# Gated cross-attention block: row maxima split by GpSimd before a single bf16 transpose, two heads later

## What is computed

```python
xn = layernorm(x)
q, k, v = xn @ Wq.T, ctx @ Wk.T, ctx @ Wv.T          # per head, D = 16
p = softmax(where(mask, q @ k.T / sqrt(D), -inf))
x = x + tanh(g_xattn) * ((p @ v) @ Wo.T + bo)
xq = fake_quant(layernorm(x), clip_x)                # one scale for all of x
h = fake_quant(silu(xq @ Wg.T) * (xq @ Wu.T), clip_down)
x = x + tanh(g_ffn) * (h @ Wd.T)
```

## Time and profile before

| | us |
|---|---|
| median of 3 runs | 254.37 |
| lowest and highest of them | 254.21, 257.52 |
| the profiled execution | 256.14 |
| its span, from first to last instruction | 254.6 |
| PE busy | 212.0 |
| DVE busy | 212.6 |
| ACT busy | 160.1 |
| POOL busy | 138.0 |

### The profile page before, as it was taken

How to read it: one execution, slowest core, us unless ns; L and a number is a source line. 1 busy time by engine, 2 the same in 40 slices (tenths; PEclk the granted TensorE clock), 3 DMA queues, 4 the chain that set the end, 5 groups by cost and what they waited for, 6 DMA issues and landing times.

```text
span 254.6 us, 5343 instructions
## 1 busy us (share of the span) xinstructions
PE 212.0 (83%) x1661; PEld 145.1 (57%) x1664; DVE 212.6 (84%) x419; ACT 160.1 (63%) x293; POOL 138.0 (54%) x241
## 2 busy tenths in 40 slices
PE   0899799979989999999999999989592898853970
PEld 0688688857746666666666666645361443312850
DVE  3378699979898998988989898969957779998992
ACT  2347476476687766667677666677726588865920
POOL 7446467643452536285675838389835433330590
PEclk9999999999999999999999999999979599996897
DMA  6999948999546653455436152000000600000296
GB/s 219 236 295 295 299 134 226 272 258 259 145 140 167 130 124 97 102 127 125 128 98 139 45 138 83 4 0 4 1 0 0 206 3 1 0 4 0 25 144 167
DMA packets 34185, 30.80 MB, mean 121 GB/s; under 512 B 5232, under 2 KB 27760, under 8 KB 34160
## 3 DMA queue, kind: packets, MB, share of 16 engines
q1 hardware_dynamic: 29776, 27.74, 40.2%
q0 software_dynamic: 1360, 1.31, 4.2%
q10 hardware_dynamic: 3024, 1.44, 2.1%
HBM read 20.65 MB, written 9.70 MB: 119 GB/s over the span
## 4 chain that ended last, share of the span: by engine, by line
PE 35%; DVE 27%; issue 10%; ACT 9%; POOL 7%; DMA 5%; SPq 4%; ACTq 0%; POOLq 0%; DVEq 0%
PE bank_o L1439 9%; PE bank_a L1422 6%; PE bank_b L1408 4%; PE bank_a L1448 3%; ACT arena L763 3%; DVE h_max L1200 3%; PE bank_a L1325 3%; DMA big<-in_ctx 3%; DVE big L1209 2%; DMA big<-max_parts 2%; DVE arena L1237 2%; DVE arena L902 2%; DVE v_all L1243 2%; POOL big L486 1%; DVE resid L917 1%
## 5 line engine op out<-in xcount | busy, mean ns | idle before, releaser
L912 DVE TENSOR_REDUCE neg_max<-bank_b 128x2 f32<-128x512 f32 x128 | 80.1, 672 | 4.9 <-PE bank_b L1314 3.0
L1422 PE MATMUL bank_a<-big 98*128 98x256 bf16 x256 | 48.8, 274 | 6.2 <-ACT arena L763 2.3
L763 ACT ACTIVATE arena<-bank_a 128x512 f32<-128x512 f32 x64 | 34.3, 605 | 13.9 <-PE bank_a L1422 13.8
L1408 PE MATMUL bank_b<-big 96*128 96x256 bf16 x224 | 42.7, 272 | 0.3 <-issue 0.2
L763 ACT ACTIVATE big<-bank_a 128x512 f32<-128x512 f32 x64 | 33.9, 595 | 12.4 <-PE bank_a L1422 12.1
L1422 PEld LDWEIGHTS bank_a<-big 98*128 98x128 bf16 x256 | 20.2, 97 | 25.4 <-issue 8.8
L1325 PE MATMUL bank_a<-arena,w_t 128*128 128x256 f32 x128 | 30.8, 387 | 0.2 <-issue 0.2
L1325 PEld LDWEIGHTS bank_a<-arena,w_t 128*128 128x128 f32 x128 | 23.6, 194 | 3.6 <-issue 0.6
L510 POOL TENSOR_TENSOR arena<-resid,arena 128x512 bf16<-128x512 f32 x16 | 18.3, 1160 | 10.7 <-ACT arena L701 10.7
L1408 PEld LDWEIGHTS bank_b<-big 96*128 96x128 bf16 x224 | 21.1, 97 | 4.5 <-issue 0.8
L570 POOL TENSOR_TENSOR x_rows<-x_rows,arena 128x256 f32<-128x256 f32 x14 | 11.6, 833 | 15.4 <-ACT arena L772 15.4
(11 more groups left out here) (179 smaller groups left out, 437.7 us busy)
## 6 DMA issues: line engine op xcount, KB each, us to landing
qk_parts<-arena SPq DMA_DIRECT2D x8, 768.0 KB, 5.5
big<-qk_parts SPq DMA_DIRECT2D x32, 192.0 KB, 3.3
big<-qk_parts SPq DMA_DIRECT2D x32, 128.0 KB, 3.3
x_rows<-in_x SPq DMA_DIRECT2D x8, 256.0 KB, 6.3
big<-qk_parts SPq DMA_DIRECT2D x32, 64.0 KB, 3.5
big<-in_ctx SPq DMA_DIRECT2D x7, 256.0 KB, 4.9
out<-x_rows SPq DMA_DIRECT2D x7, 256.0 KB, 2.8
out<-v_all POOLq DMA_DIRECT2D x5, 256.0 KB, 6.3
```

Of the source, the lines that this page charges most:

```text
L763: act.activation(probabilities(h), ring_bank(b, ("exp", h)).rearrange("p (c s) -> p c s", c=QC), ACT.Exp, scale=SCALE).then_inc(exp_done, 1)
L912: dve.tensor_reduce(neg_max[:, p, :, h], bank.rearrange("p (c s) -> p c s", c=QC), axis=AX.X, op=ALU.max, negate=True).then_inc(max_done, 1)
L1408: done = mm(to, q_st[0:KR, p, h, c * P:(c + 1) * P], k_st[0:KR, p, h], start=True, stop=not masked)
L1422: done = mm(to, k_st[0:KM, p, h, k * P:(k + 1) * P], q_st[0:KM, p, h], start=True, stop=not masked)
```

## The change

The split moves ahead of the transpose. GpSimd reads `neg_max` itself (128 rows on the partitions, 8 heads x 2 row halves = 16 values in each) and writes both bf16 parts to `max_parts`, 128 x 32 for a half. For this `neg_max` is laid out by heads, so that the 16 values lie side by side. PE does one bf16 transpose of 128x32 where it did two of f32; ACT copies 32x128 bf16 values to `max_t`; each DMA reads 16 partitions of 256 bytes where it read 8 of 512. The split now waits for DVE's reductions (and for the transpose that read the buffer before), PE waits for the split, ACT for the transpose and SP for ACT's copy. Two waits of GpSimd for the DMAs of the step before are gone. The transposes and copies stand at heads 3 and 11, where they stood at 1 and 9.

```diff
-    PE_AT = {"max_tr": 1, ("pv", 1): H + 1, ("out", 1): 2 * H + 3, "next_max_tr": 9, ("pv", 0): 9,
+    PE_AT = {"max_tr": 3, ("pv", 1): H + 1, ("out", 1): 2 * H + 3, "next_max_tr": 11, ("pv", 0): 9,
              ("out", 0): H + 11}
...
             def max_rows(b, p, half):
-                sp.wait_ge(mp_done, 2 * b + half + 1)
+                sp.wait_ge(mf_done, 2 * b + half + 1)
                 for k in range(2):
                     sp.dma_start(q_st[KR + k:KR + k + 1, p, HH * half:HH * half + HH],
-                                 max_parts[:, half, k]).then_inc(max_in[half], 16)
+                                 max_t[HH * QC * k:HH * QC * (k + 1), half]).then_inc(max_in[half], 16)
...
             def max_split(b, half):
-                pool.wait_ge(mf_done, 2 * b + half + 1)
+                heads = slice(HH * half, HH * (half + 1))
+                pool.wait_ge(max_done, H * b + HH * (half + 1))
+                if b:
+                    pool.wait_ge(mt_done, 2 * b + half - 1)
                 alone(pool)
-                chain.step(pool.tensor_copy(max_parts[:, half, 0], max_f[:, half]))
-                pool.tensor_tensor(max_parts[:, half, 1], max_f[:, half], max_parts[:, half, 0],
+                chain.step(pool.tensor_copy(max_parts[:, half, 0], neg_max[:, b % 2, heads]))
+                alone(pool)
+                pool.tensor_tensor(max_parts[:, half, 1], neg_max[:, b % 2, heads], max_parts[:, half, 0],
                                    ALU.subtract).then_inc(mp_done, 1)
...
-                    act.wait_ge(mp_done, 2 * b + half - 1)
+                    act.wait_ge(max_in[half], 32 * b)
...
-                act.activation(max_f[:, half], src[0:HH, 0:S], ACT.Copy).then_inc(mf_done, 1)
+                act.activation(max_t[:, half], src.bitcast(BF16)[0:2 * HH * QC, 0:P], ACT.Copy).then_inc(mf_done, 1)
...
-                pe.wait_ge(max_done, H * b + HH * (half + 1))
-                for c in range(QC):
-                    done = tr(to[0:HH, c * P:(c + 1) * P], neg_max[:, p, c, HH * half:HH * (half + 1)], ident_f[:])
+                pe.wait_ge(mp_done, 2 * b + half + 1)
+                done = tr(to.bitcast(BF16)[0:2 * HH * QC, 0:P], max_parts[:, half].rearrange("p k h c -> p (k h c)"), ident_b[:])
                 done.then_inc(mt_done, 1)
```

More of the change, by code:

```diff
@@ L104, in flamingo_block @@
               ("rec", 0): 13, ("means", 0): 2 * H + 13, ("back", 0): H + 3}
-    ACT_AT = {"max": 1, ("scaled", 1): 2 * H + 3, "next_max": 9, ("scaled", 0): H + 11}
-    PE_LAST = {"max_tr": 1, ("pv", 1): H + 1, ("out", 1): 2 * H + 2, ("out", 0): H + 6, ("out", 2): H + 7, ("pv", 0): 9}
-    ACT_LAST = {"max": 1, ("scaled", 1): 2 * H + 2, ("scaled", 0): H + 6, ("scaled", 2): H + 7}
+    ACT_AT = {"max": 3, ("scaled", 1): 2 * H + 3, "next_max": 11, ("scaled", 0): H + 11}
+    PE_LAST = {"max_tr": 3, ("pv", 1): H + 1, ("out", 1): 2 * H + 2, ("out", 0): H + 6, ("out", 2): H + 7, ("pv", 0): 9}
+    ACT_LAST = {"max": 3, ("scaled", 1): 2 * H + 2, ("scaled", 0): H + 6, ("scaled", 2): H + 7}
     RING, LAST = ([slot for h in range(H) for slot in (("exp", h), *(what for what, at in places.items() if at % H == h
@@ L155, in flamingo_block @@
         wd_diag = sb("wd_diag", [P, EC, P])
-        neg_max = sb("neg_max", [P, 2, QC, H])
-        max_f = sb("max_f", [HH, 2, S])
-        max_parts = sb("max_parts", [HH, 2, 2, S], BF16)
+        neg_max = sb("neg_max", [P, 2, H, QC])
+        max_parts = sb("max_parts", [P, 2, 2, HH, QC], BF16)
+        max_t = sb("max_t", [2 * HH * QC, 2, P], BF16)
         rec = sb("rec", [P, 2, NB])
@@ L587, in step @@
             def step(b, p):
-                if b:
-                    pool.wait_ge(max_in[1], 32 * b)
                 max_split(b, 1)
@@ L598, in step @@
                     scale_heads(b - 1, 1)
-                pool.wait_ge(max_in[0], 32 * (b + 1))
                 max_split(b + 1, 0)
@@ L619, in _ @@
                 step(b, b % 2)
-            pool.wait_ge(max_in[1], 32 * (B - 1))
             max_split(B - 1, 1)
@@ L911, in maxima @@
                 dve.wait_ge(a_done, H * b + h + 1)
-                dve.tensor_reduce(neg_max[:, p, :, h], bank.rearrange("p (c s) -> p c s", c=QC),
+                dve.tensor_reduce(neg_max[:, p, h], bank.rearrange("p (c s) -> p c s", c=QC),
                                   axis=AX.X, op=ALU.max, negate=True).then_inc(max_done, 1)
```

## The result

The kernel after the change takes 261.34 us (median of 4 runs, 259.33 to 262.54), against 254.80 us for the kernel before on the same chip (4 runs, 254.21 to 257.52). The ratio is 1.0243, with a 95% interval of 1.0187 to 1.03: slower by about 2.4%. The forecast was 255.0 us with a range up to 258.0. The profiled execution took 259.33 us, with a span of 257.7; that of before took 256.14, with 254.6.

A forecast was written before the change was run, and what follows sets the result against it. PE and DVE were busy some 83%; GpSimd's 14.36 us loop was taken to bound later steps, PE's order and transfers earlier ones. 0.28 - 0.33 + 1.35 - 0.25 - 0.25 + 0 - 0.25 = +0.55 on 254.37 gave 255.0 us, range 253.0 to 258.0.

The forecast's parts named there:

- the start: Before step 0: PE's first transpose waits for GpSimd's first split, so PE goes on at 64.36, +0.28 us.
- the copy: ACT's copy of the transposed maxima: falls from 0.36 to 0.25 us, bounds 0.14 and 0.36.
- the split: GpSimd's split of the maxima into two bf16 parts: 0.60 us instead of 1.11, bounds 0.58 and 1.1.
- the chain from transpose to head 8 in step 1: Transpose, exp of head 3, copy 0.25, transfer 2.53: about 3.35 us; head 8 of step 1 +1.60 us.
- the move costs cover at both places: Transposes at heads 3 and 11 stand behind the products with v; cover of 1.8 to 2.7 us, heads 0 and 8 wait.
- The transfer: DMA of the maxima, issue to PE: 2.53 us as before, at most 1.0 more.
- short runs make every transfer slower: Rival at heads 0 and 8: at +0.5 us per transfer, 6.3 us on top, 261.3 us; chance 0.05.
- So 0.25 us comes back: From step 3 GpSimd's loop is the longer; 0.25 us regained, eviction +1.05 in step 3, +0.8 in step 4.
- PE is held by GpSimd: Rival: split keeps 1.14 us, transposes at head 3 come 0.54 later in five steps, 257.4 us; chance 0.13.
- the transposes: PE: two f32 transposes of 0.31 us become one bf16 of 0.06, saving 0.25 each time where PE isn't waiting.
- DVE's chain carries this to the end: Step 7: the first products lose their transposes once more, leaving +0.55 us, which DVE's chain carries to the end.

The follow-up runs named there:

- early split: The change with GpSimd's split of the next second half moved ahead of its Newton steps and normalisation; at heads 1 and 9 with 8 partitions 252.90 us.
- the second set of runs: The change itself, unaltered, measured and traced once more: 262.18 us (ratio 1.0278).
- the early kernel at 1 and 9: The change with GpSimd's split ahead of its Newton steps and normalisation and the transposes back at heads 1 and 9, still 16 partitions: 255.8 us (1.0059).

## Why the prediction was wrong

The forecast failed in two steps, the transfer in step 0, and GpSimd's loop from step 3 on, where 0.25 us were to come back in each of two steps. By its own steps:

- **Right:** the start (the first transpose at 64.30, with PE idle 0.25 for the split, the next product at 64.45 against 64.08, +0.37 where +0.28 was forecast), the copy (0.25), the split (0.60), the chain from transpose to head 8 in step 1 (3.05 us from 88.45 to 91.50, forecast 3.35), the transfer there (2.35, forecast 2.53), and that the move costs cover at both places.
- **Failed: "The transfer" taken as 2.53 us in step 0.** It took 4.6. The forecast bounded it by the landing of other loads, as one price for all places, and did not ask what else the DMA engines carry at the place: in step 0 a store sent 1.8 us before and a fetch of instructions. The rival "short runs make every transfer slower" had the sign (over 2.7 us from issue to PE) in step 0 alone and the wrong cause: with 8 partitions the length of the run is nothing (3.11 us against 3.13), and sixteen partitions took 2.35 in step 1. That its 261.3 us is the measured median is luck. DMA: Bandwidth & Descriptors of the Trainium skill (Specifications) wants at least 512 bytes in a transfer for line rate, and its section Why small descriptors are slow exempts transfers inside SBUF. These runs agree with the exemption, as far as 4 KB can tell: 252.92 us with runs of 256 bytes and 252.90 with 512. The slow transfer and the lost cover make +3.53 at the first eviction where +1.34 was forecast. In runs in which the clock then falls, some 2.8 us more.
- **Failed: "So 0.25 us comes back" in steps 3 and 4, and nothing lost behind them.** Each of steps 3 to 6 lost 0.53 to 0.78. The forecast gave GpSimd's loop its way out by copy and transfer only. It put the projection, heads 4 to 7 and the reductions behind the held transpose, with a few tenths hidden. They are the chain: transpose, projection, eviction, weight row, exp, head 7. Term by term, from eviction to eviction in step 3: to the split's start 5.73 (before 5.70), the split 0.60 (before 1.11), from there to the products 4.45, 117.40 to 121.85 (before 3.80, 114.09 to 117.89), from the products to the eviction 4.11 (before 3.75; one more transpose stands in between now). That is +0.03 - 0.51 + 0.65 + 0.36 = +0.53. That is the rival "PE is held by GpSimd", which was right in mechanism but had the wrong condition: it doesn't need a dear split. At 0.60 for the split it is already there, since what matters is when the split ends, late behind the normalisation, and not how long it takes.
- **Mis-sized: the transposes.** 0.45 us for eight of the feed-forward part, back to back, gave 0.06 for one. Standing alone among other products it holds 0.16 to 0.23 of PE's order (95.33 to 95.49, 117.40 to 117.63). The f32 pair held 0.31 by the starts in the timeline and 0.22 in most places of the chain. So the saving is 0.15 at most and not 0.25.
- **Held by the medians: "DVE's chain carries this to the end."** 6.58 us at step 6 and 6.5 between the medians. The two profiled spans differ by only 3.1, and 2.7 of what is missing is the clock of before's trace.
- **Left out: the clock.** The forecast had granted clock 1.00 throughout and asked of no wait whether it would lower it.

A ledger by the table, in us of the medians: the kernel with nothing but the cheaper work (early split, places 1 and 9, 8 partitions) stands at 252.9, 1.9 under before (254.80). Head 1 to 3 adds 1.4, head 9 to 11 3.6, the late split 2.6, and the 16 partitions 0.9 (1.8 by the second set of runs). Before rounding that is 261.34. The traces give, up to step 6, -1.0, +1.9, +2.6, +2.2 and +1.0, together the 6.56 us between before and the change. So the change carries two costs that came together: it splits ahead of the transpose at GpSimd's old late place (2.2 to 2.6 us), and moves the transposes later to live with that (4.4 to 4.9).

What stays open: whether the store or the fetch of instructions slows the transfer from 16 partitions, and why not that from 8; and how often the clock falls in step 0 in unprofiled runs. The costs also depend on the order in which they are added, since places and hold overlap.

## What to carry to other kernels

When a job is put ahead of another on an engine with a fixed order, ask first when its engine gets to it, and follow everything that stands behind the waiting instruction through all engines back to the same place; a cheaper job in a late place can cost more than a dear one off the order. Here the same new work was a gain of 0.8% once the split stood before the normalisation, the transposes kept their cover under the products and the rows came from 8 partitions. A transfer's price is to be read at the place where it counts: the first step had a 768 KB store and a fetch of instructions beside it. And before a difference between two traces is given to a mechanism, compare the granted clock in the same stretch of both.

## What the runs showed of the hardware that was not expected

- A transfer of 2 x 4 KB inside SBUF took 4.6 to 5.2 us from issue to PE, 1 to 2 us behind a 768 KB store, from 16 partitions, and 2.5 to 3.1 from 8 partitions, with runs of 512 or of 256 bytes alike. Without the store, 16 partitions took 2.35 in step 1.
- In the traces of the change and of the early kernel at 1 and 9, the transfers from 16 partitions with a fetch of instructions (one packet, 0.02 MB) 0.8 to 2.9 us behind their first issue took up to 2.6 to 4.6 us from issue to landing; all others behind step 0 took 1.6 to 2.3.
- The granted clock fell to 0.50 after one wait of PE (1.94, 2.54 and 2.68 us in three kernels), and stayed there for up to 6 us of busy PE. It didn't in every execution: the same kernel, the same wait (2.71 and 2.68), clock 1.00 once and 0.50 once.
- Two f32 to bf16 conversions of 128x1280 on DVE took 1.14 us with GpSimd's add beside only its end, 2.30 with the bias add left out, and 4.05 us beside all of GpSimd's adds; the bias add took 1.26 to 2.24 us, the residual 0.72 to about 1.2.
- A single short bf16 transpose between other products holds three to four times what one of a row of eight does (0.16 to 0.23 us against 0.06).
